# Side work of an attention stage read from a table by score unit, in a kernel for an adaLN transformer block on one core

## The reference, cut to what matters

```python
h = layernorm(x) * (1 + ca) + sa                    # x is 1024 x 512
q = (rmsnorm(h @ wq_a.T) * w) @ wq_b.T              # 32 heads, 64 plain + 64 rotary columns
ckv, k_pe = split(h @ wkv_a.T)                      # latent of 32, rotary key of 64
kv = (rmsnorm(ckv) * w) @ wkv_b.T
scores = (q_full . k_full) * scale, causal
x = x + ga * (softmax(scores) @ v) @ wo.T
h = layernorm(x) * (1 + cb) + sb
x = x + gb * (silu(h @ gate) * (h @ up)) @ down     # inner width 1376
```

## Time and profile before

| | us |
|---|---|
| median of 3 runs | 765.67 (764.67 to 767.3) |
| profiled execution, its own time | 767.05 |
| its span | 765.3 |
| TensorE busy | 711.9 (93%) |
| VectorE busy | 526.0 (69%) |
| ScalarE busy | 289.2 (38%) |
| GpSimd busy | 231.8 (30%) |

### The profile page before, as it was taken

One profiled execution on the slowest core, in us unless ns is written; L12 is line 12 of the kernel. 1 busy time (PEld: TensorE's weight loads), 2 busy tenths in 40 slices (PEclk: granted clock), 3 DMA queues, 4 the chain that ended last, 5 costly groups with the idle time before them and its releaser, 6 DMA issues.

```text
span 765.3 us, 9320 instructions
## 1 busy us (share of the span) xinstructions
PE 711.9 (93%) x3539; PEld 480.6 (63%) x3539; DVE 526.0 (69%) x762; ACT 289.2 (38%) x427; POOL 231.8 (30%) x164
## 2 busy tenths in 40 slices
PE   3889998998999899899899899999999999999998
PEld 2755565655555565555555555555788888887886
DVE  6878689689589589689688779599695333223432
ACT  4742434434344433434343333444254322222210
POOL 2147344344254254254144220232264000000211
PEclk9999999999899999999899999999999999999999
DMA  9936621421412403403303282360200421200011
GB/s 325 240 91 167 146 49 35 102 52 32 101 23 61 100 9 76 101 0 83 83 20 83 50 302 90 112 215 6 83 19 10 114 80 55 75 11 1 27 42 41
DMA packets 40972, 63.34 MB, mean 83 GB/s; under 512 B 5536, under 2 KB 21664, under 8 KB 39072
## 3 DMA queue, kind: packets, MB, share of 16 engines
q1 hardware_dynamic: 40928, 62.75, 30.1%
HBM read 32.99 MB, written 2.10 MB: 46 GB/s over the span
## 4 chain that ended last, share of the span: by engine, by line
PE 68%; DVE 24%; issue 4%; DMA 1%; ACT 1%; SPq 0%; POOL 0%; DVEq 0%; POOLq 0%; ACTq 0%
PE PS L966 16%; DVE MX L1408 9%; PE PS L983 8%; PE PS L871 8%; PE PS L853 7%; PE PS L860 6%; PE PS L856 6%; PE PS L790 5%; DVE PR L1503 5%; PE PS L930 5%; PE PS L776 3%; PE PS L802 2%; DVE RD L1436 1%; DVE NMj L1419 1%; DVE wide L1503 1%
## 5 line engine op out<-in xcount | busy, mean ns | idle before, releaser
L1408 DVE TRANSPOSE_TENSOR_REDUCE MX<-PS 128x16 f32<-128x512 f32 x288 | 188.1, 689 | 54.3 <-PE PS L790 53.5
L1156 ACT ACTIVATE PR<-PS 128x1024 f32<-128x1024 f32 (+1 forms) x144 | 133.0, 929 | 229.2 <-PE PS L860 204.6
L790 PE MATMUL PS<-Q,KH 96*128 96x512 f32 (+1 forms) x288 | 115.5, 439 | 11.4 <-DVE MX L1408 9.4
L853 PE MATMUL PS<-Q,KH 96*128 96x512 f32 x288 | 120.2, 417 | 0.0
L860 PE MATMUL PS<-Q,KH 97*128 97x512 f32 (+1 forms) x288 | 116.1, 403 | 0.1
L856 PE MATMUL PS<-Q,KL 96*128 96x512 f32 (+1 forms) x288 | 115.8, 402 | 0.0
L1503 DVE TENSOR_TENSOR PR<-PR 128x2048 f32<-128x2048 f32 (+1 forms) x40 | 94.6, 2365 | 0.4
L790 PEld LDWEIGHTS PS<-Q,KH 96*128 96x128 f32 (+1 forms) x288 | 51.5, 189 | 67.7 <-issue 38.5
L853 PEld LDWEIGHTS PS<-Q,KH 96*128 96x128 f32 x288 | 56.3, 195 | 34.4 <-issue 17.5
L871 PE MATMUL PS<-PR,V 128*32 128x512 f32 (+3 forms) x704 | 74.5, 512 | 0.0
L1754 POOL TENSOR_TENSOR PR<-PR 128x1024 f32<-128x1024 f32 (+1 forms) x16 | 30.9, 1932 | 112.1 <-ACT PR L1156 92.7
(11 more groups left out here) (188 smaller groups left out, 1023.1 us busy)
## 6 DMA issues: line engine op xcount, KB each, us to landing
Q<-TQ SPq DMA_DIRECT2D x56, 384.0 KB, 6.1
RT<-in_wo SPq DMA_DIRECT2D x4, 1024.0 KB, 5.1
TQ<-in_wo SPq DMA_DIRECT2D x4, 1024.0 KB, 4.7
Q<-TQ SPq DMA_DIRECT2D x16, 192.0 KB, 3.4
WI<-in_gate_w SPq DMA_DIRECT2D x10, 256.0 KB, 3.4
WI<-in_up_w SPq DMA_DIRECT2D x10, 256.0 KB, 3.9
DI<-in_down_w SPq DMA_DIRECT2D x10, 256.0 KB, 2.7
PR<-in_wmod_c SPq DMA_DIRECT2D x2, 1024.0 KB, 6.3
```

The lines of the kernel that those rows point to most:

```text
L790: pe.matmul(bank, M.KH[0:rows, kt * P:(kt + 1) * P], M.Q[0:rows, g % 2, 0, f, :, qt % 4 * P:(qt % 4 + 1) * P], start=True, stop=True).then ...
L853: pe.matmul(dst, M.KH[0:KR, ks], M.Q[0:KR, w % 2, 0, qb, :, qs], start=True, stop=False)
L1156: act.activation(tiles, banks, ACT.Exp).then_inc(S_.p, 1)
L1408: dve.tensor_reduce(M.MX[:, kt, qt // 4, :, qt % 4, :], PS[:, bank_of(turn), :].rearrange("p (h s q) -> p h s q", h=HG, q=L), axis=AX.X, o ...
```

## The change

The tables of stages 0 to 6 are written out as `STAGE`, one string for each unit; `stage_table` only fills in the stage numbers. `last_table` is what is left of the planner, for stage 7, with the same places as before. The first maxima and queries (ahead of stage 0) keep their order. Nothing in the engines' programs is changed: no instruction is added or removed, only the units at which the pieces stand.

```diff
+STAGE = [
+    "p w p", "", "p p",
+    "p p", "p", "p p even0 odd0",
+    "p p", "p", "lat0 low0 split0 p",
+    "den1 p inv1", "", "p p p",
+    "p p", "p p", "p",
+    "p even1 odd1", "p p", "p p",
+    "", "p p", "",
+    "p", "p p", "p lat1 low1",
+    "", "", "split1 p p p join",
+    "", "", "",
+    "rows", "", "",
+    "norm1", "", "den0 norm0 inv0",
+]
+def stage_table(w):
+    table, part = [], 0
+    for names in STAGE:
+        entries = []
+        for name in names.split():
+            kind, half = (name[:-1], int(name[-1])) if name[-1].isdigit() else (name, None)
+            if kind == "p":
+                entries.append(("part", w + 1, part))
+                part += 1
+            elif kind in ("join", "rows"):
+                entries.append((kind, w + 1))
+            elif kind in ("den", "inv", "norm"):
+                if w >= half:
+                    entries.append((kind, w - half, half))
+            elif w < G - 2:
+                entries.append((kind, w + 2) if half is None else (kind, w + 2, half))
+        table.append(entries)
+    assert part == len(PARTS)
+    return table
-def window_table(w):
+def last_table():
...
-TABLES = [window_table(w) for w in range(G)]
+TABLES = [stage_table(w) for w in range(G - 1)] + [last_table()]
```

More of the change, by code:

```diff
@@ L372, in out_of @@
         return self.attn[:, g, qb * QB:(qb + 1) * QB]
-QUERY_PLACES = [(0.10, ("w",), 0.8), (0.26, ("even", 0), 1.2),
-                (0.29, ("odd", 0), 1.2), (0.34, ("lat", 0), 0.3), (0.36, ("low", 0), 0.9), (0.38, ("split", 0), 0.0),
-                (0.47, ("even", 1), 1.2), (0.50, ("odd", 1), 1.2), (0.55, ("lat", 1), 0.3), (0.57, ("low", 1), 0.9), (0.60, ("split", 1), 0.0)]
+STAGE = [
[31 more added lines that the diff above has]
+    return table
 WINDOW_US = 57.0
@@ L393, in group_places @@
             for place, name, busy in places]
-def window_table(w):
[L398 to L409, removed]
+def last_table():
+    w = G - 1
+    places = group_places(w, [(0.06 + 0.1 * m, ("fold", m), 1.3) for m in range(G)])
+    places += group_places(w, [(0.3 + 0.3 * n, ("gate", n), 2.5) for n in range(2)])
+    places += group_places(w, [(0.84 + 0.06 * st, ("high", st), 0.0) for st in range(2)])
+    places += group_places(w, [(0.40 + 0.10 * d, ("mod", 2, d), 0.6) for d in range(KD)])
+    places += [(0.15, ("den", w - 1, 1), 0.7), (0.16, ("inv", w - 1, 1), 0.8), (0.24, ("norm", w - 1, 1), 0.0)]
     places += [(0.42, ("den", w, 0), 0.7), (0.43, ("inv", w, 0), 0.8), (0.50, ("norm", w, 0), 0.0)]
@@ L424, in window_table @@
         table.append(names)
[L425 to L431, removed]
     for n in range(NUNIT):
```

## The result

The changed kernel takes 722.1 us (median of 4 runs, 721.88 to 722.38), the kernel before 766.48 in the same set: ratio 0.942, interval 0.938 to 0.945. 731 was forecast, 724 to 747 was the range. The direction and the places were right, and the gain, 44.4 us, is more than the 38.7 us that the prediction had as all there was to remove.

What follows compares the result with a forecast made beforehand. TensorE was taken as the bound, held at places by VectorE. 767.05 - 13.5 (join) - 14.6 (banks) - 10.6 (dips) + 1.0 (stage 0) + 3.2 (lock) = 732.6, or 731 for the runs' median; range 724 to 747 us.

Steps and rivals of the forecast that it cites:

- The walk: New order stepped through with profiled durations: join 0.8 us ahead of TensorE's need, banks back 0.6 to 0.8 us early.
- the chain over the stage's edge: From `den0` through `norm0` and `weights_low` to unit 5's projection: 6.5 us against 7.1 to 7.8 of TensorE, no cost.
- B: Rival: bank waits come back elsewhere, two meetings of an add with GpSimd a stage, 11 us, giving 742; chance 0.27.
- C: Rival: the join is held by GpSimd's `split_low`, making rows and the following add late, 8.5 us, giving 740; chance 0.08.
- E: Rival: slower, as GpSimd instructions behind adds delay unit 5's projection, 7.7 us a stage, giving 774; chance 0.06.
- Clock, -10.6: Dips to the 1.2 GHz level after the join wait in stages 1 to 5 all go, saving 10.6 us.
- The rule behind it: Clock dips follow TensorE waits of over 2 us; a dip without such a wait ahead would overthrow the clock term.
- the removable part is 38.7: TensorE's waits and dips: 13.5 (join) + 14.6 (banks) + 10.6 (dips) us, taken as all there was to remove.
- The lock, +3.2: Step 7's add meets GpSimd's `split_low`: unit 33 waits 0 or 1.3 us in stages 1 to 5; half taken, +3.2.
- Stage 0, +1.0: Fold of the weights at unit 0 waits in stage 0 for the weights' DMA, +1.0 us, once.

Runs made afterwards that it cites:

- the fill: Kernel before, with 10 bfloat16 matmuls of 512 columns nobody reads, ahead of the transposition's wait for the join in stages 0 to 6: 759.4 us (0.989).
- the rest alone: Changed kernel with maxima parts, `join` and `rows` back at the units of the kernel before; fold, queries and denominators as changed: 754.5 us (0.982).
- `rows` at 27: Changed kernel with `rows` moved from unit 30 to unit 27: 749.6 us (0.977 to the kernel before).
- `split1` at 27: Changed kernel with `split1` moved from unit 26 to unit 27: 744.7 us (0.974 to the kernel before).
- the two halves of the change: Against the kernel before: only maxima parts, join and rows moved, 744.2 us; only fold, queries and denominators moved, 754.5 us.

## Why the prediction was wrong, point by point

- *Where TensorE loses time, and that the new order takes the waits away*: right. The walk's margins came out close: join 0.72 (0.8 predicted), `split_low` ending just as the add is due, the chain over the stage's edge 1.2 us early (`weights_low` ends at 193.47, the projection starts at 194.66; "about one"). B, C and E did not come. B was near: the queries at their old units bring waits back and cost 24.4 us.
- *Clock, -10.6*: right in cause (the fill) and size (filled, the five windows take 285.7 instead of 294.8 us, which is four dips, 9.1; stage 6 with the fifth is 1.9 shorter once the fill's 2.3 are taken off; 11.0 in all). The rule behind it, that only a wait of over 2 us is followed by a dip, is too simple (the dip in stage 0 with the rest alone); the time did not hang on that.
- **The step that failed**: "Without waits and dips a stage is 57.17 - 4.55 = 52.6 us of TensorE", and with it "the removable part is 38.7". The listed waits were taken as all of the lost time. A stage is 51.38, so 1.24 us a stage were missed, 6.2 us over stages 1 to 5, and about one more in stage 6: waits behind a 0.40 us record lose 0.17 more than listed, the start after the next is 0.1 late, and a second wait for a bank within the next record is listed for the weight load alone. The prediction's own costs of units, parts and projections, with the value steps and their gaps (estimated at 10.6), two denominators (1.9) and the fold (0.5), add up to 36 x 0.70 + 36 x 0.233 + 6 x 0.70 + 10.6 + 1.9 + 0.5 = 50.8, nearer to 51.4 than to 52.6. It did not make that sum. Its own sign of being right, "windows between transpositions near 52.6 to 54", failed with it.
- *The lock, +3.2*: no wait at unit 33 came of it. The end taken as one of two equals, that GpSimd's queued instruction goes first, is not what the runs show: an add that waits gets in ahead of it (4.38 in the experiment). In the changed kernel the add was hardly late at all.

  The Trainium skill (SBUF — State Buffer, "Who interferes with whom") has whoever issues first hold the shared pair of ports for its whole instruction, which agrees with that 4.38. It also says that on trn2 a `tensor_reduce` never contends, which agrees with the join: 1.60 beside `split_low`, 1.61 with hardly any overlap.
- *Stage 0, +1.0*: the wait for the weights is listed as 0.46 and is 0.67 by starts (85.60 to 86.50, where 0.23 is due). A wait of 0.26 for the maxima's DMA just ahead of it is 0.17 more by starts than before. Together about 0.8.
- In numbers: 732.6 - 7.3 (missed: 6.2 in stages 1 to 5, 1.1 in stage 6, its dip among it) - 3.2 (lock) = 722.1 for the profiled execution, measured 721.9. That stage 0 with what lies around came out within 0.2 is partly luck: its own hidden waits, which the sum left out too, are offset by small things around it, the 0.4 us ahead of the stage among them. The 1.4 us taken off for the runs' median was no property of the change: the changed kernel's profiled execution lies 0.2 from its median.
- *The range* ended at 724. All of the 38.7 with nothing for the lock and for stage 0 gives 767.05 - 38.7 - 1.4 = 727, so only 3 us below the sum's best case were allowed for terms larger than thought, and 4% were left below that.

What stays open: why the same wait is followed by no dip, a short or a long one, and the 0.2 us or so of stage 0's edge. In the four runs with such waits (the kernel before, the rest alone, `rows` at 27, `split1` at 27) every long dip (6.8 us) begins before the wait is over, 0.3 to 1.5 us ahead of its end; a short one (3.4 us) begins between 0.2 us before that end and 1.8 after it.

## What to carry to other kernels

Read lost time of a pipelined engine from start to start, not from the idle that a trace lists: here four listed waits of 4.55 us were 5.8 us of starts. As a check, add the pure steps of a stage; if they come out below "window less waits", the rest is hidden waiting.

Waits on one engine pair are not additive: removing only the bank waits made the join wait longer, and the two halves of the change gave 24 and 14 us alone and 44 together. An ordered table should be judged by where the last of the serving engine's work ends.

A wait of two us that stands alone may cost another one to three through the clock. Filling it with matmuls into the bank that is about to be written brought 9.2 us against the kernel before of the same set, for two lines of code. In the other sets that kernel's median was 1.6 to 4.1 us lower.

## What the runs showed of the hardware beyond that

- The spread of the kernel before (759.8 to 769.7 us) is gone where the long waits are gone: 721.8 to 722.4 for the changed kernel, 758.9 to 760.3 for the filled one. For 38 executions of the kernel before the mean granted clock is known, and the time goes with it: 0.994 at 759.8 us, 0.989 at 764.5, 0.981 at 769.4. So the spread is one of the clock; that it is the number and length of the dips is the likely reading, as only one of them has a trace here.
- Of 25 idle waits of 2.1 to 3.2 us in four runs, 23 were followed by a stretch at 0.50 to 0.51 of the full clock. Waits of 0.81 to 0.83 (seven), 1.23, 1.38 and 1.47 were not, but one of 1.02, 4.6 us behind one of 1.42, was. The length of a wait alone does not decide it.
- An SBUF-to-SBUF add that waits for a GpSimd instruction starts as that one ends, ahead of the GpSimd instruction queued behind (4.38 = 2.2 + 2.2), and that one then waits for the add (3.31 and 3.33 instead of 1.28).
